# A graph network's gather passes walked in two banks, with one TensorE update per group and lookups built from broadcast types

## The reference

```python
h = relu(layernorm(x))
# layer 0, RGCN, 10 relations, twice: mean over each (destination, relation), then a weight per relation
etype = argmax(edge_attr_42[:, 16:-16], axis=1)
seg   = dst * 10 + etype
sums  = segment_sum(h[src], seg, N * 10);  cnt = segment_sum(ones, seg, N * 10)
mean  = (sums / max(cnt, 1)).reshape(N, 10, -1)
out   = einsum('nrd,rdo->no', mean, w_rel) + h @ root + bias
# layer 1: hr = einsum('ni,rio->rno', h, weight)
out   = relu(segment_sum(hr[edge_type_3, src] * edge_weight[:, None], dst, N))
# layer 2, SAGE, twice: mean over all edges of a destination (degree = number of edges)
agg   = segment_sum(h[src], dst, N) / max(deg, 1)[:, None];  out = agg @ Wl.T + bl + h @ Wr.T
# layer 3, SchNet filter
Wij   = (ssp(edge_attr_20 @ W1 + b1) @ W2 + b2) * edge_weight[:, None]
agg   = segment_sum((h @ W_in2f)[src] * Wij, dst, N)   # with src and dst as given to the filter layer
```

## Time and profile before

| | us |
|---|---|
| median of 3 runs | 18,265.93 |
| lowest and highest run | 18,255.7 and 18,277.25 |
| span of the profiled execution | 18,422.2 |
| five gather stretches (passes 1 to 5, from the first gather of each to the last add, about) | 2756.61, 2427.33, 2428.24, 2434.77, 2609.64 |
| filter pass | 3153.30 |

### The profile page before, as it was taken

How to read it: one execution, slowest core, us unless ns; L and a number is a source line. 1 busy time by engine, 2 the same in 40 slices (tenths; PEclk the granted TensorE clock), 3 DMA queues, 4 the chain that set the end, 5 groups by cost and what they waited for, 6 DMA issues and landing times. The chain is left out here.

```text
span 18422.2 us, 189911 instructions
## 1 busy us (share of the span) xinstructions
PE 8433.5 (46%) x37745; PEld 6706.7 (36%) x37746; DVE 7139.1 (39%) x33414; ACT 2442.5 (13%) x4374; POOL 11077.2 (60%) x11347
## 2 busy tenths in 40 slices
PE   2464444463333343333343333333333377777777
PEld 1233333333333333333332332322222355555555
DVE  7644444432222232222232222255555534444443
ACT  0120000020000020000020000000000044444443
POOL 0045555636666646666636666566666448888883
PEclk9975555585555565555565555555555567777775
DMA  2131111131111131111121111123333246666665
GB/s 85 64 123 40 40 39 39 40 146 55 45 45 45 45 100 45 45 45 45 45 66 45 45 45 45 49 80 84 83 84 84 73 95 118 118 117 118 117 117 122
DMA packets 981246, 1326.79 MB, mean 72 GB/s; under 512 B 201421, under 2 KB 635620, under 8 KB 981180
## 3 DMA queue, kind: packets, MB, share of 16 engines
q0 software_dynamic: 552016, 851.84, 21.1%
q1 hardware_dynamic: 429208, 474.72, 8.9%
HBM read 992.21 MB, written 333.54 MB: 72 GB/s over the span
## 5 line engine op out<-in xcount | busy, mean ns | idle before, releaser
L588 POOL DMA_INDIRECT rows<-table_dram,row_st x8320 | 8018.1, 964 | 3188.8 <-issue 2894.6
L734 PE MATMUL ps<-tab_s,rows 128*128 128x128 f32 x16640 | 4123.4, 427 | 6939.1 <-DMA rows<-table_dram,row_st 4302.8
L734 PEld LDWEIGHTS ps<-tab_s,rows 128*128 128x128 f32 x16640 | 3604.2, 320 | 7432.5 <-issue 7386.0
L570 POOL DMA_INDIRECT agg_dram<-acc,sum_row x1664 | 2646.9, 1591 | 529.0 <-issue 383.7
L997 DVE TENSOR_TENSOR acc<-ps,acc 128x128 f32 x2080 | 605.5, 291 | 5685.4 <-PE ps L734 4010.6
L1038 DVE TENSOR_SCALAR tab_s<-iota,rw_st 128x128 f32<-128x128 f32 x6656 | 1787.8, 361 | 11.5
L734 PE MATMUL ps<-scratch,tab_s 128*128 128x128 f32 x3328 | 669.0, 366 | 821.8 <-DVE scratch L1182 791.5
L583 POOL COPY row_st<-row_i 128x8 int32 x1040 | 210.5, 202 | 1262.7 <-PE ps L734 1072.4
L734 PEld LDWEIGHTS ps<-scratch,tab_s 128*128 128x128 f32 x3328 | 596.8, 269 | 871.7 <-issue 871.3
L548 POOL DMA_DIRECT2D table_dram<-tab_s x200 | 106.6, 533 | 1179.9 <-ACT tab_s L671 917.4
L635 ACT ACTIVATE yT<-acc 128x512 f32 x75 | 46.9, 626 | 4899.5 <-DVE acc L997 4893.7
(11 more groups left out here) (182 smaller groups left out, 10596.4 us busy)
## 6 DMA issues: line engine op xcount, KB each, us to landing
scratch<-in_src_row SPq DMA_DIRECT2D x832, 256.0 KB
rows<-table_dram,row_st POOLq DMA_INDIRECT x8320
table_dram<-tab_s POOLq DMA_DIRECT2D x200, 640.0 KB, 3.2
scratch<-in_dst_row SPq DMA_DIRECT2D x416, 256.0 KB
scratch<-table_dram SPq DMA_DIRECT2D x416, 64.0 KB
agg_dram<-acc,sum_row POOLq DMA_INDIRECT x1664
scratch<-agg_dram SPq DMA_DIRECT2D x100, 256.0 KB, 3.8
x_dram<-xn_h SPq DMA_DIRECT2D x75, 256.0 KB, 2.4
```

The costliest lines, as they stand in the source:

```text
L570: pool.indirect_dma_start(agg_dram[j], bass.IndirectOffsetOnAxis(ap=sum_row[:, QUAD * q + j:QUAD * q + j + 1], axis=0), sums[:, q, j * P:( ...
L588: pool.indirect_dma_start(rows[:, u, :], None, table_dram[p["rels"]], bass.IndirectOffsetOnAxis(ap=row_st[:, u:u + 1], axis=0)).then_inc(r ...
L734: pe.matmul(o, lhs[:, u, :], rhs[:, u, :], start=j == 0 or not summed, stop=j == QUAD - 1 or not summed).then_inc(mm_done, 1)
```

## The change

The gather passes go a whole group deep.

- `walk` runs the groups as a first one, a loop over pairs, and a last one. Rows, one-hots, `row_st`, `rw_st` and the sums (`ps[0]`, `ps[1]`, a quad per 128 columns) stand in two banks.
- POOL (`gather`, L625 to L630) waits for `row_staged` and for `group_mm` of the group two before, and issues 16 gathers. DVE makes the copy of row numbers (`stage_rows`, L1106), after it has added the group before (`add_group`, L1141 to L1145).
- PE signals once per group (`gathered_products`, L807) and DVE once per quad of one-hots. `mm_done`, `add_done` and `hot_ready` count quads, in COUNT and FILTER too.
- LOOKUP without transposes in the loop: the prologue transposes `etype` once (13 PE transposes, 13 ACT copies) and stores it to `type_dram`. In the pass SP loads it broadcast, a quad at a time, in two buffers; ACT turns it into one-hots by two activations (Abs, then Relu); PE looks up a group ahead (`look_up`, L822), and DVE fuses destination one-hot and product in one `scalar_tensor_tensor` per tile (L1159).
- The degree lookup moves to pass 2 (`look_up_degrees`, four matmuls and 16 fused steps a group).
- `set_windows` precedes `stage_rows(0)`, so POOL's first gather of a pass comes after it. A memset of `xn_h` is gone.

The diff, cut to its core:

```diff
+        def walk(e, body):
+            body(0, 0, 0, True, ngroups == 1)
+            middle = max(ngroups - 2, 0) // 2
+            if middle:
+                with e.Fori(0, middle) as i:
+                    body(i * 2 + 1, 1, i, False, False)
+                    body(i * 2 + 2, 0, i + 1, False, False)
+            for g in range(1 + 2 * middle, ngroups):
+                body(g, g % 2, g // 2, False, g == ngroups - 1)
...
 @block.sync
+                    with sp.Fori(0, reps) as r:
+                        with sp.Fori(0, ngroups) as g:
+                            for q in range(4):
+                                sp.wait_ge(relT_ready, (r * ngroups + g) * 4 + (q + 1))
+                                settle(sp)
+                                sp.dma_start(type_row[:, q % 2, :], type_dram[bass.ds(g * GROUP + q * QUAD, QUAD), :]
+                                             .rearrange("t e -> (t e)").unsqueeze(0).broadcast_to([P, BANK])
+                                             ).then_inc(type_in[q % 2], 16)
...
 @block.gpsimd
-                        for part in range(2):
-                            pool.wait_ge(mm_done, used + (part + 1) * (GROUP // 2))
-                            pool.tensor_copy(row_st[:, us[0]:us[-1] + 1],
-                                             row_i[:, bass.ds(g * GROUP + us[0], GROUP // 2)]).then_inc(row_staged, 1)
-                            pool.wait_ge(row_staged, turn * 2 + (part + 1))
+                    def gather(g, bank, i, first, last):
+                        pool.wait_ge(row_staged, (reps * k + r) * (ngroups + 1) + g + 1)
+                        pool.wait_ge(group_mm, turn + (3 - apart))
+                        for q in range(4):
+                            for u in range(QUAD * q, QUAD * (q + 1)):
+                                pool.indirect_dma_start(
+                                    row_banks[bank][:, u, :], None, table_dram[p["rels"]],
+                                    bass.IndirectOffsetOnAxis(ap=row_st[:, bank, u:u + 1], axis=0)
+                                ).then_inc(row_in[bank][q], 16)
...
 @block.scalar
-                                act.activation(rel_hotT[:, q % 2, :], ps[4][:], ACT.Copy).then_inc(relT_ready, 1)
+                                act.wait_ge(type_in[q % 2], turn * 32 + 16 * (q // 2 + 1))
+                                act.wait_ge(relT_ready, n + (q + 2))
+                                act.activation(yT[:], type_row[:, q % 2, :], ACT.Abs, bias=rel_of[:, 3:4]).then_inc(relT_step, 1)
+                                act.wait_ge(look_mm, turn * 2 + (q // 2 + 1))
+                                act.wait_ge(relT_step, n + (q + 1))
+                                act.activation(rel_hotT[:, q, :], yT[:], ACT.Relu, bias=ones[:, 0:1], scale=-1.0
+                                               ).then_inc(relT_ready, 1)
...
 @block.tensor
+                for q in range(4):
+                    pe.wait_ge(hot_ready, base + (q + 5))
+                    pe.wait_ge(row_in[bank][q], landed + 64)
+                    for u in range(QUAD * q, QUAD * (q + 1)):
+                        mm = pe.matmul(ps[bank][:, q * P:(q + 1) * P], rows[:, u, :], hot[:, u, :],
+                                       start=u % QUAD == 0, stop=u % QUAD == QUAD - 1)
+                mm.then_inc(group_mm, 1)
...
 @block.vector
+                    def add_group(g, done, bank):
+                        dve.wait_ge(group_mm, done)
+                        for q in range(4):
+                            window = acc[:, bass.ds(win[q], P)]
+                            dve.wait_ge(add_done, base + (q + 4))
+                            dve.tensor_tensor(window, ps[bank][:, q * P:(q + 1) * P], window, ALU.add).then_inc(add_done, 1)
...
+                                i = dve.scalar_tensor_tensor(out=out(u), in0=iota[:], scalar=rw[:, 0, u:u + 1],
+                                                             in1=looked_up(j), op0=ALU.is_equal, op1=ALU.mult,
+                                                             accum_out=wout_st[:, u:u + 1])
...
+                        if not first:
+                            add_group(g - 1, gathers + 2, 1 - bank)
+                        stage_rows(g + 1, 1 - bank)
```

More of the change, by code:

```diff
@@ L555, in _ @@
                 wait_stores(pool, k)
[L556 to L558 removed]
+                if PASSES[k + 1] == FILTER:
                     with pool.Fori(0, reps) as r:
@@ L832, in run_pass @@
                                 quad_products(base, q, same, P, msg, summed=False)
+                    if kind in (LOOKUP, PLAIN):
+                        walk(pe, gather_group)
+                    else:
+                        with pe.Fori(0, ngroups) as g:
+                            group(g)
+            pe.wait_ge(type_ready, 1)
+            for c in range(n_attr):
+                n = min(P, ntiles - c * P)
+                if c >= 4:
+                    pe.wait_ge(typeT_ready, c - 3)
+                pe.matmul(ps[c % 4][0:n, 0:P], etype[:, c * P:c * P + n], ident[:],
+                          start=True, stop=True).then_inc(typeT_mm, 1)
+            pe.wait_ge(typeT_ready, n_attr)
             run_pass(0)
@@ L920, in _ @@
             step(dve.memset(wt_deg[:], 0.0))
+            step(dve.memset(row_i[:, ntiles:ntiles + GROUP], 0))
             dve.wait_ge(made, 13)
@@ L1008, in run_pass, with stage_rows, one_hots @@
                     set_windows(pn, r)
-                    with dve.Fori(0, ngroups) as g:
+                    def stage_rows(g, bank):
+                        dve.tensor_copy(row_st[:, bank, :], row_i[:, bass.ds(g * GROUP, GROUP)]).then_inc(row_staged, 1)
+                    if kind != COUNT:
+                        dve.wait_ge(rows_ready, sum(q in (0, 2, 3) for q in range(pn)))
+                        stage_rows(0, 0)
+                    def one_hots(q, hot_of):
+                        for j in range(QUAD):
+                            i = hot_of(QUAD * q + j)
+                        i.then_inc(hot_ready, 1)
@@ L1119, in run_pass @@
-                        if kind == LOOKUP:
-                            dve.wait_ge(hot_ready, base + GROUP)
-                            for full, w in ((wt_a, 0), (wt_deg, 1)):
-                                part = full[:, bass.ds(g * GROUP, GROUP)]
-                                dve.tensor_tensor(part, wout_st[:, w, :], part, ALU.add)
+                        dve.tensor_copy(rw_st[:, 1, :], etype[:, bass.ds(g * GROUP, GROUP)]).then_inc(rw_staged, 1)
+                        dve.wait_ge(rw_staged, turn * 2 + 2)
```

429 lines of the change are left out of this document (229 added, 200 removed).

## The result

The changed kernel took 18,446.44 us (median, 18,422.65 to 18,448.53) against 18,260.82 us (18,251.92 to 18,277.25): a ratio of 1.0095, 95% interval 1.0081 to 1.0110. It is slower by 0.95%, where 16,510 us was forecast. The span is 18,446.8 us.

What follows compares the result with a forecast made beforehand. POOL's issuing of gathers was taken to bound the kernel: span 18,422.2 − 1966 + 171 + 41 = 16,668 us, less 156 from span to median, rounded to 16,510 us; range 16,280 to 17,200, the forecast's own 16,300 to 16,780.

Steps and rivals of the forecast that it cites:

- theory S: Experiments' theory, slow chips: while POOL streams gathers, each engine sends something per instruction, one per 0.70 us tick, updates queuing too.
- the 12.3 us: Delay before PE's four updates of a quad came through while POOL streamed gathers; read as about 3 us per update.
- The floor of a gather: POOL in the five gather passes: 1.285 us per gather if it never waits, 20.56 us per group, 10,691 us in all.
- −1966: Gain in the five gather passes, in us, from POOL never waiting once its row-number copies go to DVE.
- 14 us of slack: Plain passes: room left after products, adds and staged rows, some 6.5 us into the next group's 20.6 us of gathers.
- Part 2: PE's updates fall from 16 to 1 a group, DVE's one-hots' from 16 to 4; no gain of its own booked.
- Part 3: First pass: the new LOOKUP chain takes 12 us per group beside POOL's 20.6 us, so it costs nothing.
- rival B: First pass: LOOKUP's chain takes POOL's place, 24 to 26.5 us per group, total about 17,000 us; chance 0.12.
- Part 4: Second pass: the degree lookup adds under 6 us per group on DVE, under POOL's 20.6 us; costs nothing.
- Part 5: Fifth pass: DVE's work, serial waits and late updates take 22.2 us per group, +171 us on POOL's floor.
- Part 6: Starts and ends of passes: later first gathers +31 us, adds in series +6, prologue +4; filter pass nothing.
- C: Rival, slower: PE's update held while POOL streams, then adds and staged rows follow; 6.1 us per group, 19,535 us; chance 0.07.

Runs made afterwards that it cites:

- e4: Changed kernel with short POOL stops put back, one per group in the third pass, three in the fourth: 2438.40 and 2401.69 us, against 2417 and 2432 us.
- e3: Changed kernel with updates nobody waits for put back, PE's in the third pass, PE's and DVE's in the fourth: 2432.94 and 2435.14 us, against 2417 and 2432.
- the first comparison: Complete changed kernel against the kernel before, on slow chips: 18,446.44 against 18,260.82 us, ratio 1.0095.
- e8: Kernel before, unchanged, traced again on a slow chip: 18,263.95 us, with a span of 18,262.2 us.

## Why the prediction was wrong

**What bounds the kernel.** That POOL's issuing sets the pace is right on a quick chip alone, and there no update is late. On a slow one both kernels stand on the slow path, and POOL's copies and waits filled time that was not POOL's to use (e4: 218 us of stops put back, and the pass no longer). By theory S the 0.13 us of the earlier trace rows and the 12.3 us of the earlier trace rows are the same line empty and full.

**The floor of a gather (the step that failed).** 1.285 us × 1664 × 5 = 10,691 us; measured 10,518 on a quick chip (1.257 to 1.27 us per gather) and out of reach on a slow one, where gathers alone need 2303 us per pass and the whole plain pass 2423 to 2464. The two terms for the five passes, −1966 and +171 us, came to +115 there. The trace held a sign of it: the 12.3 us were read as three per update. By theory S what stood in line were the instructions of a quad, eight matmuls and eight weight loads, and 16 × 0.70 = 11.2 us is near the 12.3; no run shows this for that quad. The change removes hardly any of them (PE 3320 + 3320 per plain pass on either side). The 14 us of slack fell for the same reason: the single update came up to 24 us late.

**Part 2.** Booked at nothing, which is right (e3: within 16 us). Its reasoning, that fewer updates come sooner, is refuted: a single one came 23.8 us late. On a quick chip (timeline, third pass) the adds begin 0.25 us after PE's last product of the group (7019.33 + 2.05):

```profile
7019.33 2.05 PE L807 MATMUL ps<-scratch 128*128 128x128 f32 x8 [2.99 <-DMA scratch<-table_dram,row_st]
...
7021.63 1.57 DVE L1145 TENSOR_TENSOR acc<-ps,acc 128x128 f32 x4 [14.07 <-PE ps L807]
```

By the rule of the Trainium skill ("TensorE: Matmul & The Clock Gate", the section on the per-tile semaphore tail) an increment is through in well under a microsecond. The trace of a quick chip agrees, with 0.25 us; that of a slow chip, with 23.8 us, doesn't.

**Part 3, LOOKUP.** The chain stays under POOL on a quick chip (2095.13 us), as forecast, and rival B is out there. On a slow chip the pass gains 161 us, but at 2555.24 us, 24.6 per group, it shows B's sign: over 2400 us, with 976.4 us of idle time ahead of L1159, 697.0 of them put down to "remote" (page of the first comparison; 57.2 us on a quick chip). The plain passes take 23.3 there, so most of that is the common slow path; whether a chain of LOOKUP's own adds the last 1.3 us no run shows.

**Part 4, degree lookup.** Forecast nothing; on a quick chip right (2097.74), on a slow one +144 to +156. Free time of DVE was taken for free instructions.

**Part 5, fifth pass.** Forecast 2309 us; 2115.80 on a quick chip, where no update is late and the term of +171 is nothing, and 2650.48 on a slow one. There POOL's waits for `row_st` are, in the list of waits of that pass,

```profile
POOL scratch L630 <- DVE row_st L1106: 282.1, 47, 15.8
POOL rows L630 <- DVE row_st L1106: 275.2, 46, 15.7
```

557 us. The copy now stands behind DVE's 76 instructions of a group (7888/104), and DVE is the engine that steps. Gathers took 964 to 967 ns in this pass, so the shared port of the Trainium skill ("GPSIMD Engine Reference", "Specifications") again cost at most 0.2 us per group, not 4.6.

**Part 6.** +41 forecast, 42 measured outside the passes on one slow chip, and 34 on quick ones: 16,309.9 − 10,518.0 us on chip 4 against 17,202.0 − 11,444.3 on chip 15.

**The sum.** The subtraction of 156 us from span to median was a mistake of its own: e8 has 1.8 us between its span and its time, and the profiled execution most likely came from a slower chip than the timed ones. That 16,289 us on a quick chip lies near the forecast of 16,510 is luck. The kernel before takes 17,195 us there, so the gain is 906 us where 1756 were forecast, for the 1262.7 us of waits ahead of the copies are not there to be gained.

**The rivals.** C named the right place (late update, adds, staged rows, POOL stopped) and the right sign, with 0.07. Its price was off: not 6.1 us in each group but 10 us in each second or third, and by the gathers' own limit, 22.1 against 20.6 us, a part of the forecast gain is lost even with no stop.

## What to carry to other kernels

When updates are late, count what the signalling engine executes in the time, not what it signals: a constant step between instructions that neither wait nor signal is the sign, and a busy share says nothing of it. Then look whether the trace is whole: a releaser "remote" or a missing time to landing on one chip, where another has both, says that records were lost, and that the profile itself may be in the way. If removing known costs of an engine moves nothing (two copies of 0.7 us a group, here), look for a limit by leaving out all other work beside it: the gathers alone at 1.384 us, on such a chip, would have told before any rewriting. And a trace is of one chip; a forecast for a kernel whose waits look odd wants a trace from a second one.

## What the runs showed of the hardware

- In these executions, all of them recorded, chips of one kind differ: the same kernel took 17,184 to 17,204 us on three and 18,245 to 18,423 us on three others, with equal granted clock in the plain passes (0.50) and equal times of single instructions (a gather 0.96 us on both).
- On a slow chip PE, DVE, ACT and POOL all fall into steps of 0.70 us while gathers stream and for some 7 us after (7548.03 to 7555.16), ACT with copies of 0.10 us that wait for nothing. After such a stop the lateness starts again from little: in the third pass of the first comparison an update 22 us or more late is followed by one that is 0.2 to 3.5 us late.
- The steps begin behind a stretch at full pace: nine one-hots on DVE, and 184 gathers on POOL when it runs alone.
- Where the steps are, the trace loses records of semaphore updates: a slow chip's holds 21,311 to 34,802 of the 133,120 landings that the gathers signal, a quick chip's 132,816 or more.
- With no work beside them, gathers of 128 rows take 1.384 us on a slow chip and 1.257 on a quick one; with 64 rows beside all other work, the time on a slow chip is as with 128 (2483 and 2464 us), on a quick one 2020 against 2104.
